# Attention written in slots of an image pair, with GpSimd normalising the softmax and keys without zero padding

## What is computed

```python
# layer 0: attention with 8-channel queries and keys, per image
q = relu(x @ wq + bq); k = relu(x @ wk + bk); v = x @ wv + bv
out = softmax(q @ k.T) @ v + x
# layer 1: group norm (32 groups), then attention with 64 channels
h = group_norm(y); w = softmax((h@Wq) @ (h@Wk).T * 64**-0.5)
y = y + (w @ (h@Wv)) @ Wo
# layer 2: each token attends to its 7 neighbours of a hexagonal grid, 8 heads
score = sum over a head's channels of q * shifted k ; softmax over 7
```

## Time and profile before

| | |
|---|---|
| time, median of 3 runs | 128.46 us |
| span of the profiled execution | 125.2 us |
| the rest of the median, outside that span | 3.3 us |
| TensorE busy | 105.7 us (84%) |
| VectorE busy | 93.7 us (75%) |
| ScalarE busy | 68.5 us (55%) |
| GpSimd busy | 42.7 us (34%) |
| share of the chain that ended last | TensorE 42%, VectorE 29%, ScalarE 15%, issue 8% |
| DMA | 2.81 MB, mean 22 GB/s |

### The profile page before, as it was taken

How to read it: one execution, slowest core, us unless ns; L and a number is a source line. 1 busy time by engine, 2 the same in 40 slices (tenths; PEclk the granted TensorE clock), 3 DMA queues, 4 the chain that set the end, 5 groups by cost and what they waited for, 6 DMA issues and landing times.

```text
span 125.2 us, 1845 instructions
## 1 busy us (share of the span) xinstructions
PE 105.7 (84%) x600; PEld 64.4 (51%) x600; DVE 93.7 (75%) x246; ACT 68.5 (55%) x164; POOL 42.7 (34%) x43
## 2 busy tenths in 40 slices
PE   4988999899999988599399957998697992998990
PEld 1475957577777775365035634985353530221350
DVE  1078999878888669737979989793878739998733
ACT  3137985687979775637503310025534579986530
POOL 8996004351608217095500079991000000000000
PEclk9999999999999999999999999999999999999999
DMA  3960000000000000000000000000000000000022
GB/s 105 309 280 0 0 0 0 5 5 0 0 0 0 0 5 0 0 0 0 5 0 0 0 3 0 0 0 0 0 0 0 0 5 3 0 0 0 5 84 84
DMA packets 1593, 2.81 MB, mean 22 GB/s; under 512 B 176, under 2 KB 1200, under 8 KB 1584
## 3 DMA queue, kind: packets, MB, share of 16 engines
q1 hardware_dynamic: 1152, 2.02, 4.5%
q10 hardware_dynamic: 432, 0.67, 1.6%
HBM read 2.17 MB, written 0.52 MB: 22 GB/s over the span
## 4 chain that ended last, share of the span: by engine, by line
PE 42%; DVE 29%; ACT 15%; issue 8%; DMA 2%; POOL 1%; ACTq 0%; DVEq 0%
PE bank L913 5%; DVE strips L307 5%; PE bank L883 4%; DVE probn L604 4%; ACT prob L411 4%; PE bank L1074 3%; PE bank L1104 3%; DVE ffh L253 3%; PE bank L1116 3%; PE bank L1052 3%; ACT strips L529 3%; DVE nmax L595 3%; DMA p<-in_p 2%; PE duo L1140 2%; DVE qkprod L738 2%
## 5 line engine op out<-in xcount | busy, mean ns | idle before, releaser
L411 ACT ACTIVATE prob<-bank,nmax 128x256 f32<-128x256 f32 x32 | 14.8, 469 | 8.2 <-DVE nmax L595 7.8
L883 PE MATMUL bank<-kz,q 128*128 128x256 f32 x64 | 16.4, 383 | 0.3 <-ACT kz L400 0.3
L595 DVE TENSOR_REDUCE nmax<-bank 128x2 f32<-128x512 f32 x16 | 11.0, 689 | 5.7 <-PE bank L883 5.7
L307 DVE COPY strips<-strips 32x480 f32<-32x480 f32 x32 | 12.8, 400 | 3.0 <-ACT strips L529 2.4
L883 PEld LDWEIGHTS bank<-kz,q 128*128 128x128 f32 x64 | 11.5, 190 | 2.1 <-issue 0.5
L604 DVE TENSOR_SCALAR probn<-prob,rrec 128x256 f32<-128x256 f32 x32 | 12.1, 421 | 0.6
L529 ACT ACTIVATE strips<-bank,bnsh 32x512 f32<-32x512 f32 x16 | 10.9, 680 | 2.1 <-PE duo L1140 1.1
L893 PE MATMUL bank<-pv,probn 128*128 128x128 f32 x64 | 10.0, 278 | 2.1 <-DVE probn L604 2.1
L501 ACT ACTIVATE sq<-bank,cb 128x512 f32<-128x512 f32 x4 | 2.7, 687 | 15.3 <-PE bank L1074 11.0
L1140 PE MATMUL duo<-strips,ctaps 128*32 128x512 f32 x72 | 8.3, 596 | 3.2 <-DVE strips L307 3.2
L893 PEld LDWEIGHTS bank<-pv,probn 128*128 128x128 f32 x64 | 7.4, 142 | 4.6 <-DVE probn L604 4.2
(11 more groups left out here) (148 smaller groups left out, 229.3 us busy)
## 6 DMA issues: line engine op xcount, KB each, us to landing
p<-in_p SPq DMA_DIRECT2D x1, 952.0 KB, 7.1
xT<-in_xT SPq DMA_DIRECT2D x4, 128.0 KB, 4.0
p<-in_p ACTq DMA_DIRECT2D x1, 448.0 KB, 5.7
out_dram<-xT SPq DMA_DIRECT2D x1, 256.0 KB, 2.0
out_dram<-xT SPq DMA_DIRECT2D x2, 128.0 KB, 1.7
pv<-in_pv ACTq DMA_DIRECT2D x1, 128.0 KB, 3.2
p<-in_p ACTq DMA_DIRECT2D x1, 79.5 KB, 3.0
```

The costliest lines, as they stand in the source:

```text
L307: return engine.tensor_copy(strips[32 * s:32 * s + 32, c % 2, r, :, 1:1 + SIDE, d], strips[32:64, c % 2, r, :, 1:1 + SIDE, f])
L411: s.activation(prob[:, n % 3, b, :], S_BANK[n % 3][:, b * TOK:(b + 1) * TOK], ACT.Exp, bias=nmax[:, n, b:b + 1], accum_out=rsum[:, n, b:b ...
L595: v.tensor_reduce(nmax[:, n, :], S_BANK[n % 3].rearrange("p (b m) -> p b m", b=BLK), AX.X, ALU.max, negate=True).then_inc(max_ready, 1)
L883: ins = mm(S_BANK[n % 3][:, b * TOK:(b + 1) * TOK], q[:, b * 128:b * 128 + 128], k, start=True, stop=True)
```

## The change

- The loops run over 8 slots, each an image pair of one layer. Slots 0 to 3 are layer 0.
- `scores(m)` makes both images of the pair. Each contraction runs over the image's own 32 partitions (layer 0) or 64 partitions (layer 1) of queries and keys. The keys have no zeros, their two memsets go, and each group of keys is written by one instruction: VectorE for layer 0, ScalarE for layer 1.
- Each image has its own score bank, four in all. `W_BANK` becomes one bank, which holds queries and keys side by side.
- The multiplication by the reciprocal sums goes to GpSimd, as `tensor_scalar` with two operations, of which the second multiplies by 1.0. The border instructions get the same second operation.
- The rest of the group norm goes to GpSimd too. VectorE negates the mean for it.
- The second image's copy of the transposed probabilities goes from ScalarE to VectorE.
- GpSimd's memset of `strips` moves from the start to behind the key products.
- `project2` and the key products come behind the last slot. The split of `w1` goes into slot 7, and the cast of `head_cast` between the products of pairs 0 and 1.

```diff
-        S_BANK = bank[0:3]
-        T_BANK = bank[3:5]
-        O_BANK = bank[5]
-        W_BANK = bank[6:8]
+        S_BANK = bank[0:4]
+        T_BANK = bank[4:6]
+        O_BANK = bank[6]
+        W_BANK = bank[7]
...
         @block.gpsimd
-            g.memset(flat(kz0[:, :, :]), 0.0).then_inc(zeroed, 1)
-            g.memset(flat(kz1[:, :, :]), 0.0).then_inc(zeroed, 1)
-            g.memset(strips[:, :, :, :, :, :].rearrange("p a b c d e -> p (a b c d e)"), 0.0)\
-                .then_inc(zeroed, 1)
...
+            def border(buf, k, h):
                 g.tensor_scalar(buf[:, 2 * h:2 * h + 2, :, :].rearrange("p a b c -> p (a b c)"),
-                                zeros[:, :], col("in_proj_b", k), None, ALU.add).then_inc(kv2_border, 1)
+                                zeros[:, :], col("in_proj_b", k), 1.0, ALU.add, ALU.mult).then_inc(kv2_border, 1)
+            def normalise(m, i):
+                n = 2 * m + i
+                pool.wait_ge(rrec_ready, n + 1)
+                if m >= 2:
+                    pool.wait_ge(probT_ps, n - 3)
+                for b in range(BLK):
+                    ins = g.tensor_scalar(probn[:, n % 4, b, :], prob[:, n % 4, b, :], rrec[:, n, b:b + 1], 1.0,
+                                          ALU.mult, ALU.mult)
+                ins.then_inc(norm_done, 1)
+            def group_norm(j):
+                pool.wait_ge(gvar_ready, 2 * j + 2)
+                g.tensor_tensor(grs[:, j:j + 1], gvar[:, j:j + 1], minus_half[:, 0:1], ALU.pow).then_inc(gn_step, 1)
...
+                g.tensor_scalar(hT[:, j, :], yT[:, j, :], gsc[:, j:j + 1], gbi[:, j:j + 1],
+                                ALU.mult, ALU.add).then_inc(h_ready, 1)
+            border(k2, 1, 0)
+            border(k2, 1, 1)
+            for m in range(NATT):
+                normalise(m, 0)
+                normalise(m, 1)
+                if m == 0:
+                    border(v2, 2, 0)
+                    border(v2, 2, 1)
+                if 2 <= m < 2 + PAIRS:
+                    group_norm(m - 2)
...
             for j in range(PAIRS):
                 pool.wait_ge(q2_sb, j + 1)
                 pool.wait_ge(k2_sb, j + 1)
                 for r in POOL_RUNS[j]:
                     ins = key_product(g, j, r)
                 ins.then_inc(prod_pool, 1)
+            g.memset(strips[:, :, :, :, :, :].rearrange("p a b c d e -> p (a b c d e)"), 0.0)\
+                .then_inc(zeroed, 1)
...
         @block.scalar
+            for m in range(NATT):
+                if 4 <= m < 4 + PAIRS:
+                    values1(m - 4)
+                exps(m, 0)
+                exps(m, 1)
+                if 3 <= m < 3 + PAIRS:
+                    keys_queries1(m - 3)
+                copy_probT(m)
+            for j in range(PAIRS):
+                keys_queries2(j)
+                values2(j)
...
         @block.vector
+            def copy_probT(m):
+                dve.wait_ge(probT_ps, 2 * m + 2)
+                if m >= 2:
+                    dve.wait_ge(pv_ps, m - 1)
+                v.tensor_copy(flat(probT[:, 2 * (m % 2) + 1, :, :]), T_BANK[1]).then_inc(probT_dve, 1)
...
+            keys0(0)
+            values0(0)
+            for m in range(NATT):
+                maxes(m, 0)
+                if m:
+                    copy_probT(m - 1)
+                maxes(m, 1)
+                if m == 0:
                     keys0(1)
                     values0(1)
+                if 2 <= m < 2 + PAIRS:
+                    group_variance(m - 2)
+                inverse_sums(m, 0)
+                if m:
+                    residual(m - 1)
+                inverse_sums(m, 1)
+                if 1 <= m < 1 + PAIRS:
+                    stats(m - 1)
...
+                if m == 7:
                     dve.wait_ge(tables_in["p2"], 16)
                     v.tensor_copy(w1_hi[:, :], table["w1T"]).then_inc(w1_split, 1)
...
+            copy_probT(NATT - 1)
+            key_products(0)
+            residual(NATT - 1)
+            dve.wait_ge(consts, 1)
+            v.tensor_copy(flat(head_cast_r[:, :, :]), flat(head_cast[:, :, :])).then_inc(cast_r, 1)
+            for j in range(1, PAIRS):
+                key_products(j)
...
         @block.tensor
+            def scores(m):
+                if m >= 2:
+                    pe.wait_ge(exp_done, 2 * BLK * (m - 1))
+                if m < PAIRS:
...
+                    own = [slice(64 * (m % 2) + 32 * i, 64 * (m % 2) + 32 * i + 32) for i in range(2)]
                 else:
...
+                    own = [slice(64 * i, 64 * i + 64) for i in range(2)]
                 for b in range(BLK):
-                    ins = mm(S_BANK[n % 3][:, b * TOK:(b + 1) * TOK], q[:, b * 128:b * 128 + 128], k,
-                             start=True, stop=True)
+                    for i in range(2):
+                        ins = mm(S_BANK[2 * (m % 2) + i][:, b * TOK:(b + 1) * TOK],
+                                 q[own[i], b * 128:b * 128 + 128], k[own[i], :], start=True, stop=True)
                 ins.then_inc(scores_ps, 1)
...
             def attend(p):
-                pe.wait_ge(probT_sb, 2 * p + 2)
+                pe.wait_ge(probT_act, p + 1)
+                pe.wait_ge(probT_dve, p + 1)
...
+                    pe.wait_ge(attn_out, p)
+                    pe.wait_ge(gstats_sb, min(p, PAIRS))
...
+            for m in range(NATT):
+                scores(m)
+                if m == 0:
+                    project0(1)
+                    project0_values(1)
+                if 4 <= m < 4 + PAIRS:
+                    project1_values(m - 4)
+                if 2 <= m < 2 + PAIRS:
+                    group_stats(m - 2)
+                if m:
+                    transposes(m - 1, 1)
+                if 3 <= m < 3 + PAIRS:
+                    project1(m - 3)
+                if m:
+                    attend(m - 1)
+                if m == 1:
+                    prepare()
+                transposes(m, 0)
+            for k in range(3):
+                project2(0, k)
+            transposes(NATT - 1, 1)
+            for k in range(3):
+                project2(1, k)
+            attend(NATT - 1)
...
+            head_sums(0)
             head_sums(1)
```

More of the change, by code:

```diff
@@ L263, in build @@
         block = ctx.enter_context(nc.Block())
[L270 to L273, removed]
+        NATT = 2 * PAIRS
+        L0_BANKS = (bank[6], bank[7])
+        V0_BANKS = (bank[5], bank[4])
         PREP_BANK = bank[3]
@@ L280, in build @@
         WARM_UP, WARM_SOFTMAX, WARM_SOFTMAX2 = 1, 2, 1
[L281 to L288 removed]
+        PROJ2 = [(bank[7][:, 0:TOK], bank[7][:, TOK:2 * TOK], bank[0][:, 0:TOK]),
+                 (bank[1][:, 0:TOK], bank[2][:, 0:TOK], bank[3][:, 0:TOK]),
+                 (bank[7][:, 0:TOK], bank[0][:, 0:TOK], bank[1][:, 0:TOK]),
+                 (bank[2][:, 0:TOK], bank[3][:, 0:TOK], bank[0][:, 0:TOK])]
         POOL_RUNS = [(0, 2), (0, 2), (2,), (2,)]
@@ new lines, in group_norm @@
+            def group_norm(j):
+                pool.wait_ge(gvar_ready, 2 * j + 2)
+                g.tensor_tensor(grs[:, j:j + 1], gvar[:, j:j + 1], minus_half[:, 0:1], ALU.pow).then_inc(gn_step, 1)
+                pool.wait_ge(gn_step, 3 * j + 1)
+                g.tensor_tensor(gsc[:, j:j + 1], grs[:, j:j + 1], col("L1_conv_gn_scale"), ALU.mult)\
+                    .then_inc(gn_step, 1)
+                pool.wait_ge(gn_step, 3 * j + 2)
+                g.tensor_scalar(gbi[:, j:j + 1], gmv[:, j, 0:1], gsc[:, j:j + 1], col("L1_conv_gn_bias"),
+                                ALU.mult, ALU.add).then_inc(gn_step, 1)
+                pool.wait_ge(gn_step, 3 * j + 3)
+                g.tensor_scalar(hT[:, j, :], yT[:, j, :], gsc[:, j:j + 1], gbi[:, j:j + 1],
+                                ALU.mult, ALU.add).then_inc(h_ready, 1)
@@ L1000, in head_sums @@
                 ins.then_inc(hexs_ps, 1)
-            for n in range(SLOTS):
-                if n < NATT:
-                    scores(n)
-                if n == 2:
+            for m in range(NATT):
+                scores(m)
+                if m == 0:
                     project0(1)
-                if n == 3:
                     project0_values(1)
-                if n in (5, 7, 9, 11):
-                    group_stats((n - 5) // 2)
-                if n in (7, 9, 11, 13):
-                    project1_values((n - 7) // 2)
-                if 2 <= n <= NATT:
-                    transposes(n - 2)
-                if n == NATT:
-                    transposes(n - 1)
-                if n == PREPARE:
-                    prepare()
-                if 4 <= n <= NATT and n % 2 == 0:
-                    attend((n - 4) // 2)
-                if n == NATT:
-                    attend(n // 2 - 1)
-                if n in (6, 8, 10, 12):
-                    project1((n - 6) // 2)
-                if n in QK2_SLOTS:
-                    project2(QK2_SLOTS.index(n), 0)
-                    project2(QK2_SLOTS.index(n), 1)
-                if n == V2_SLOTS[-1]:
```

(16 more changed lines are left out.)

286 lines of the change are left out of this document (100 added, 186 removed).

## The result

The changed kernel takes 140.45 us (median of 4 executions, 139.12 to 143.18), the kernel before 128.48 beside it. The ratio is 1.0867, with an interval of 1.0794 to 1.0939: slower by 12 us, where the forecast said 2.3.

The account below looks back on a forecast made before the run. Bound by a loop of waits across engines in attention, then by key products. Slots, normalisations and key products put the first softmax maximum at 66.81 us, 2.3 later; added to the median: 130.8 us, range 127.0 to 137.5.

Parts of the forecast that it names:

- N: Time of one GpSimd normalisation in attention, the forecast's unknown: taken as 0.50 us, ends 0.22 and 0.75.
- The 0.38: Alternative estimate in us of one GpSimd normalisation, from 1.8 cycles an element at 1.2 GHz; total would be 128.8.
- the rival at the border's rate: GpSimd normalisations as slow per element as the border instruction, 0.75 us each: total 136.5 us, chance 0.20.
- Row tiles side by side: Attention scores of both images overlap on separate array rows: 0.87 us a pair plus 0.10 for shape changes.
- Periods: Length of each attention slot's chain: 5.01 + 2N in slots 4 and 5, 4.48 + 2N in slots 2 and 3.
- Turns of the key products: After attention, VectorE and GpSimd key products alternate instead of overlapping, so durations add: 12.45 us.
- First maximum: Start of the first softmax maximum after the second head sums: 58.81 + 16N, so 66.81 us against 64.51 before.
- The rest carried over: Span behind the first softmax maximum, 60.7 us, assumed unchanged.
- The 3.3 us between span and median: Gap between the profiled span of 125.2 and the median of 128.46 us, carried over unchanged.
- the removed 7.0 us of TensorE's work: Scores shed by TensorE, 8 x 0.87 us, listed in favour of the faster rival (quick GpSimd, chance 0.30).

Follow-up runs that it names:

- the run with zeros: Changed kernel plus matmuls on zeros in TensorE's waits, two in slot 0, one each in slots 1 and 2: median 132.97 us, profiled execution 130.58.

## Why the prediction was wrong

**The sign held, the size did not, and the time fell outside the range.** The chain, point by point:

- *N*, taken 0.50 from the affine select of the earlier trace rows: 0.485 on average, 0.94 for two. Right. The 0.38 worked out from the Trainium skill (GPSIMD Engine Reference, section 3.1) was not reached. The border with its second operation took 0.81 for 648 elements instead of 1.91, so that choosing another row than the border was right and the rival at the border's rate was not.
- *Row tiles side by side*: right, 1.06 between starts at full clock (7.06 to 8.12 in the change) against 0.97.
- *Periods*, 5.01 + 2N in slots 4 and 5, so 5.95 at N = 0.47: 6.06 each in the run with zeros (29.43 to 41.55). Slot 0 took 5.71 (7.61 to 13.32) instead of 5.43, slots 1 to 3 took 16.04 (13.32 to 29.36) instead of 15.43. From scores(0) to the first key product it is 54.28 - 7.61 = 46.7 instead of 37.39 + 16N = 44.9: 1.8 us too short, in small pieces everywhere.
- *Turns of the key products*, 12.45: 66.24 - 54.28 = 12.0. The mechanism was right (six products on two engines 6.05, on one 4.23), the size 0.5 too large.
- *First maximum*, 66.81: 68.06 with the clock held (scores(0) came 0.5 us late there, at 7.61 instead of 7.12), 77.21 in the change itself (scores(0) at 7.06).
- *The rest carried over*: 60.7 us of span behind the maximum was 60.64 with the clock held, 62.19 in the change.
- *The 3.3 us between span and median*: a misreading. Span and time of one and the same execution of the kernel before differ by 1.74 to 1.93 us in all 53, and by 1.85 and 1.88 in the profiled ones of the change and of the run with zeros (by up to 2.73 in other versions). The other 1.45 or so is clock: the profiled execution had 1.00, the median one 0.985.

**The step that failed** is the one that took the durations of the earlier trace rows and of the whole of TensorE's work as they stood at full clock, and carried the rest over "unchanged". The change takes three quarters of the rows from the first scores and puts a wait of 1.89 us behind them, and TensorE ran at 1.2 GHz from behind 12 to about 37 us. Up to the first maximum the clock cost 9.15 us, a piece of it at the second head sums, and behind it 1.55. Neither the sum nor a rival had a term for the clock. The profile of before held two clues. The 3.3 us that nobody accounted for meant that the kernel already lost its clock somewhere in most executions. And the removed 7.0 us of TensorE's work, listed as an argument for a gain, helped to keep the clock up: given back as full rows, it left the clock at 1.00 up to 70 us in the profile, behind the same wait.

That the run with zeros lands on 130.58, 0.2 from the forecast of 130.8, is luck: the maximum is 1.25 later than forecast, and 3.3 us were added where 1.88 belong. The two errors cancel.

**What stays open**: why one program gets 1.00 in one execution and 0.96 in the next; zeros in one more wait moved the share of such executions, but no run explains it. How far the rows and how far the wait of slot 0 bring the clock down is shown by small counts only. How the 3.9 us of GpSimd divide was measured only near 0.973, where the turns account for 1.5 to 2.5 and the normalisation for 2.4 to 2.9; at full clock the division was not measured.

## What to carry to other kernels

A change that takes work from TensorE, in time or in rows, or that puts a wait into it, has to be priced at both clock levels: look up what stands around each new wait, and read the granted clock before any duration. Products of zeros on full rows in such waits cost nothing on the path of slot 0 and took 7.5 us off the median here. Before summing, compare the profiled execution with the median one: here their spans differed by the clock, and the difference was carried over as if it were fixed. And two engines that took turns were slower than one.

## What the runs showed of the hardware

- Behind the same wait of 1.9 us, scores on 32 rows (computed twice) left mean clocks of 0.884 and 0.885 in two of four executions, while scores on full rows of about the same length left none below 0.963.
- The clock falls in some executions of a program and not in others: a wait of 2.43 us at 103 us stands in a profile at 1.00 and in one at 0.985.
- Filling that wait of 2.43 us raised the executions at 0.998 or above from 3 of 10 to 11 of 12, and brought the median from 127.66 to 126.33 us.
- Separate score groups on neighbouring 32-row tiles overlap without being interleaved in the program: twelve instructions in 1.27 us.
- GpSimd's tensor_scalar with one operation took 1.91 us for 648 elements, with two operations 0.81, though it does more.
